# Two pieces of output weights behind the copies of queries, and the clearing of the key buffers tied to the updates: a cross-attention kernel on one core

## What is computed

```python
w     = softmax(x @ rW.T + rb)                       # 8 experts
a_sum = x @ lora_A.T                                 # 64 values
upd   = sum_n w[n] * (a_sum @ lora_B[n].T)
h     = nan_to_num(x + 0.5 * upd)                    # clipped to +-1e4
Q, K, V = h @ Wq.T + bq, ctx @ Wk.T + bk, ctx @ Wv.T + bv
attn  = softmax(where(mask, Q K^T / sqrt(32), -inf))
y     = h + (attn V) @ Wo.T + bo
out   = (y - mean(y)) / sqrt(var(y) + 1e-5) * ln_g + ln_b
```

## Time and profile before

| what | value |
|---|---|
| median of 3 runs | 639.76 us (639.5 to 642.15) |
| the profiled execution's own time | 639.82 us |
| its span | 638.0 us |
| PE busy | 628.6 us, 99% of the span |
| DVE busy | 498.2 us, 78% |
| ACT busy | 337.6 us, 53% |
| POOL busy | 268.0 us, 42% |
| granted TensorE clock | full speed in nearly all of the 40 slices |
| HBM | 67.29 MB read, 46.14 MB written |

### The profile page before, as it was taken

The page is one execution under the profiler, slowest core; times in us unless marked ns, Lnnn a source line. Parts: engine busy times, 40 slices in busy tenths (PEclk is TensorE's granted clock), DMA queues, the critical chain, the costliest instruction groups (busy, mean ns, idle before and its releaser), DMA issues.

```text
span 638.0 us, 10730 instructions
## 1 busy us (share of the span) xinstructions
PE 628.6 (99%) x3455; PEld 544.4 (85%) x3455; DVE 498.2 (78%) x907; ACT 337.6 (53%) x999; POOL 268.0 (42%) x358
## 2 busy tenths in 40 slices
PE   9999999999999999999999999999999999999995
PEld 8988889888988889888788888888888888888884
DVE  5789995578457773677568899999999999999834
ACT  5453453123242232323258777777778777777621
POOL 0120001000030002000325556788899888888956
PEclk9999999999999999999999999999999999999998
DMA  8945595436874467721857993534355354523132
GB/s 316 408 127 173 176 300 190 155 83 205 241 253 160 115 221 246 279 98 38 269 129 282 373 389 107 149 94 148 115 127 179 97 175 111 150 99 117 59 107 100
DMA packets 103399, 114.14 MB, mean 179 GB/s; under 512 B 57008, under 2 KB 76080, under 8 KB 103344
## 3 DMA queue, kind: packets, MB, share of 16 engines
q1 hardware_dynamic: 103008, 113.07, 53.9%
q10 hardware_dynamic: 336, 0.39, 0.2%
HBM read 67.29 MB, written 46.14 MB: 178 GB/s over the span
## 4 chain that ended last, share of the span: by engine, by line
PE 96%; DVE 2%; issue 1%; DMA 0%; ACT 0%; POOL 0%; DVEq 0%; POOLq 0%; ACTq 0%
PE ps L602 26%; PE ps L603 26%; PE ps L604 26%; PE ps L664 4%; PE ps L747 4%; PE ps L760 2%; PE ps L761 2%; PE ps L636 1%; PE ps L638 1%; PE ps L635 1%; PE ps L674 1%; DMA stage<-WkT 0%; DVE u_lo L891 0%; DVE cx_sum L987 0%; PE ps L627 0%
## 5 line engine op out<-in xcount | busy, mean ns | idle before, releaser
L1268 POOL TENSOR_TENSOR u_sb<-a_sb,w_sb 128x512 f32<-128x512 f32 x16 | 19.6, 1246 | 235.3 <-DVE w_sb L885 230.4
L602 PE MATMUL ps<-wo_hi,cx_hi 128*128 128x512 f32 (+1 forms) x264 | 105.9, 401 | 0.0
L1194 ACT ACTIVATE s_sb<-s_sb,s_min 128x64 f32<-128x64 f32 x256 | 85.8, 339 | 34.6 <-DVE s_min L965 34.6
L604 PE MATMUL ps<-wo_hi,cx_lo 128*128 128x512 f32 (+1 forms) x264 | 101.7, 385 | 0.0
L603 PE MATMUL ps<-wo_lo,cx_hi 128*128 128x512 f32 (+1 forms) x264 | 101.6, 385 | 0.0
L602 PE MATMUL ps<-act_hi,w_hi 128*128 128x512 f32 x256 | 100.9, 394 | 0.3 <-DVE q_sb L939 0.3
L603 PE MATMUL ps<-act_lo,w_hi 128*128 128x512 f32 x256 | 99.9, 390 | 0.0
L604 PE MATMUL ps<-act_hi,w_lo 128*128 128x512 f32 x256 | 99.8, 390 | 0.0
L1159 ACT ACTIVATE act_hi<-h_t 128x512 fp32r<-128x512 f32 x32 | 20.3, 633 | 111.6 <-DVE h_t L928 111.6
L987 DVE SCALAR_TENSOR_TENSOR cx_sum<-ps,bias_c,cx_raw 64x256 f32<-64x256 f32 x128 | 61.8, 483 | 8.8 <-ACT cx_raw L1208 4.8
L1279 POOL TENSOR_TENSOR s_sb<-s_sb,s_inv 128x512 f32<-128x512 f32 x64 | 67.1, 1048 | 0.0
(11 more groups left out here) (120 smaller groups left out, 1538.9 us busy)
## 6 DMA issues: line engine op xcount, KB each, us to landing
q_cols<-q_sb SPq DMA_DIRECT2D x32, 512.0 KB, 3.6
qb<-q_cols SPq DMA_DIRECT2D x64, 256.0 KB, 3.9
x_sb<-xT SPq DMA_DIRECT2D x32, 256.0 KB, 3.0
h_rows<-hn_sb SPq DMA_DIRECT2D x64, 128.0 KB, 3.0
output_weights<-wo_sb SPq DMA_DIRECT2D x32, 256.0 KB, 2.7
z_sb<-h_rows SPq DMA_DIRECT2D x16, 512.0 KB, 4.5
out<-z_sb SPq DMA_DIRECT2D x15, 512.0 KB, 2.9
stage<-WvT SPq DMA_DIRECT2D x8, 512.0 KB, 4.7
```

The source lines that it names most:

```text
L602: pe.matmul(dst, lh, rh, start=(first and j == 0), stop=False)
L604: mm = pe.matmul(dst, ll, rh, start=False, stop=(last and j == n - 1))
L1194: act.activation(s_sb[c % 4][:, h, :], s_sb[c % 4][:, h, :], ACT.Exp, bias=s_min[c % 2][:, h:h + 1], scale=-1.0, accum_out=s_sum[c % 2][:, ...
```

## The change

In batches 1 and 2 the seventh piece of output weights no longer stands beside query block 6, ahead of the copies of the queries, but behind them with the eighth. And stage `zero` is no longer between the phases but ahead of `("flush", 3, 6)`, so that ACT's key loads come ahead of its last `add_bias`; POOL's memsets wait for the last update's matmuls (`up_mm`) instead of for the last clipping.

```diff
@@ first_phase
-            for n in range(KC - 1):
+            for n in range(KC - 2):
                 beside[i][n] += [("output_weight", KC * (i - 1) + n)]
...
             if i == NB - 1 and n == 1:
-                return out
+
+                at_flush = out.index(("flush", i, KC - 2))
+                return out[:at_flush] + [("zero",)] + out[at_flush:]
         out += leave(i, 0, 0) + leave(i, 0, 1)
         if 0 < i < NB - 1:
-            out += [("output_weight", KC * i - 1)]
+            out += [("output_weight", KC * i - 2), ("output_weight", KC * i - 1)]
@@ run
-    for what, *index in first_phase() + [("zero",)] + second_phase():
+    for what, *index in first_phase() + second_phase():
@@ zero, on POOL
-                pool.wait_ge(bound_ready, ALL)
+
+                pool.wait_ge(up_mm, ALL)
```

## The result

| | before | after |
|---|---|---|
| median of 20 runs each | 640.34 us | 638.88 us |
| lowest to highest | 639.5 to 642.38 us | 638.27 to 640.27 us |
| span of the profiled execution | 638.0 us | 636.9 us |

The ratio of after to before is 0.9973, with a 95% interval from 0.9965 to 0.9981: 1.7 us faster, between 1.2 and 2.3. It is the ratio of the means; the medians lie 1.46 us apart, since six of the runs of the kernel before lie above 641 us and none of the changed one. I had forecast no change at all, 639.8 us, and so missed a gain that is clear of the noise. The measured median is inside the range and nearest to the rival "no collision", 638.9 us. But the collision took place. The rows tell what came of it.

A forecast was written before the change was run, and what follows sets the result against it. PE was taken to bound the kernel, with 96% of the chain of waits. Output weights -0.64 us plus +0.6 us from the first scores to chunk 4 gave 0.0 us, so 639.8 us, range 638.4 to 641.0.

The forecast's parts named there:

- no collision: Rival: last update's memset and DVE's finite and bound do not clash, first scores start on time; 638.9 us, chance 0.36.
- the collision: At the last update, POOL's third memset shuts out DVE's finite or bound; forecast case 639.8 us, chance 0.47.
- What can be gained at most: PE's stops at batches 1 and 2's second query halves and at the first scores: 1.04 us, 0.16% of the span.
- part 1: Seventh piece of output weights moved behind the query copies: 0.32 us stop gone in batches 1 and 2, -0.64 us.
- Part 2, the collision: Memsets start at about 305.2, 307.0 and 308.7; the third makes DVE's bound of the last update 1.8 us late.
- turns: At the third memset, one of DVE's two instructions slips in at 308.8; the second waits until about 310.9.
- Part 3, the knock-on to the key loads: On ACT, act_hi ends at 313.5, key loads issue 0.3 us later; first scores stop 0.7 us or more, not 0.40.
- What is queued behind: SP stands still 1.5 us before the last h rows; chunk 4's queries land at 334.0, its scores 0.6 us later.
- The SP rival: SP becomes the bound at chunk 4's scores: queries land at 336.0, 2.6 us late; 641.8 us, chance 0.12.
- The sum: Whole kernel: -0.64 from the output weights, +0.6 from first scores to chunk 4, 0.0 us; time stays 639.8 us.
- the collision case: Forecast case with DVE shut out by the third memset: 639.8 us, bounds 639.4 to 640.4, chance 0.47.

The follow-up runs named there:

- Experiment 1: Kernel before with only the seventh piece of output weights moved behind the query copies; memsets and key loads as before: 639.24 us, ratio 0.9982.
- Experiment 5: Changed kernel, but the third memset waits for the last clipping again, the first two stay early: 638.8 us, ratio 0.9976 to the kernel before.
- Experiment 3: Kernel before with only the memsets made early, waiting for the last update's matmuls; key loads stay behind the last add_bias: 641.16 us, ratio 1.0015.
- Experiment 4: Kernel before with only the key loads moved ahead of the last add_bias; memsets still behind the last clipping: 640.03 us, ratio 0.9998.
- experiment 7: Changed kernel with three more loads on SP ahead of the values, waiting for each other: 646.57 us, ratio 1.0095 to the kernel before.

## Why the prediction was right and wrong

- **What can be gained at most** ("1.04 us, 0.16% of the span"): mis-sized. The places were right, all three, and nothing else moved. But I counted the late start of the first matmul only, 0.32 us, and called 1.04 us the most that the change can bring; it brought 1.5 to 1.7. Between two marks with only the first stop between them (the first matmul behind batch 2's transposes of u, and the first behind batch 3's adapter) lie 248.18 - 183.34 = 64.84 us before and 248.04 - 183.72 = 64.32 us after: **0.52 us for a stop**. Behind a stop the next matmul follows after 0.34 us, not 0.23 (186.82 behind 186.48): in a full stream a matmul's weights are loaded beside the matmul ahead of it, and here that load began only 0.11 us after the stopped one, at 186.59. A few hundredths more are lost in the matmuls that follow. At the first scores it is 0.49 us. So part 1 was worth 1.0 us where I had 0.64, and all three 1.5. Experiment 1 measured part 1 at 1.2 us, interval 0.5 to 1.7. The prediction also said that a measurement of this kernel can't tell less than 0.5%, 3.2 us, from no change; with 20 runs of each kernel the interval is 0.5 us to either side, and 1.7 us is well clear of it.
- **Part 2, the collision**: right in place, kind and size (1.67 us for 1.8). Only my "turns" were wrong: it was `finite`, not `bound`, that waited. The two came to the same moment: in all five profiles with the three memsets early and together, the record of `finite` starts at most 0.02 us ahead of that of the third memset, and each time the memset went first. Why it did is not shown. Experiment 5 removed the wait by removing the overlap, so the cause is shown. The row that carried it, DVE and POOL beside each other in the earlier trace rows, was the right one to go by, and the Trainium skill's rule ("SBUF — State Buffer", section "Who interferes with whom") holds in this case: a memset, which only writes, shut out a tensor_scalar until it had ended, 2.10 us against 0.43.
- **Part 3, the knock-on to the key loads**: this is the step that failed. "With DVE 1.8 us late, `act_hi` ends at 313.5, and the loads are issued 0.3 us later than before." They were issued 0.34 us earlier. ACT does not wait for the end of the instruction ahead of a transfer. 0.65 us of error, and with it the sign of the part: the stop went instead of growing. The rows of before could have told: there the loads started 0.08 us after the second memset had ended (311.30 + 1.81 = 313.11), and 0.02 us before `add_bias` had ended by its row (312.48 + 0.73 = 313.21). Experiments 3 and 4 settled it: memset in 4, start of `add_bias` in 3.
- **What is queued behind**: the place was right, the size not. SP paused for 0.38 us instead of 1.5: `add_bias` started 0.65 us sooner than I had it, by the same mistake, and SP itself arrived 0.45 us later, since its two `qb` issues ahead took longer. Then it made up more than it had lost. The stop of 0.6 us ahead of chunk 4's scores was 0.0. That chunk 4's queries are the point where SP would become the bound is shown by experiment 7, and by the 0.22 us that a weight load waited there.
- **The rival "no collision"** gave the right time by luck: its -0.64 was too small by 0.4 us, and its premise did not hold. **The SP rival** did not occur; experiment 7 shows that its mechanism exists and lacks only the delay.
- **The sum**: the two errors both hid a gain, 0.4 us in part 1 and 1.1 us in the rest, together the 1.5 us that I called zero. That the median still lies inside 638.4 to 641.0 is no merit of the mechanism: the range was wide enough for the rival. (Its bounds for the collision case, 639.4 and 640.4, come out at 639.5 and 640.3 by their own terms.)
- **The gaps of PE**: ahead of the prediction "gaps of some 9 us in all" are named. 7.5 us of them lie behind the last matmul (630.5 to 638.0), where DVE, POOL and ACT finish the last rows, 1.2 us ahead of 104.54, and only 0.7 us in all that is between. So the three stops were nearly all that PE's idle time still held there.

Not settled: why the last key load lands 0.6 to 1 us sooner in some profiles. It was not tried to hold the order of the issues on both queues fixed. So how often the stop at the first scores returns in either kernel is known from a few profiles only.

## What to carry to other kernels

Price a stop of a full TensorE by the distance between two marks around it, not by the idle time in front of one matmul: here 0.32 us of late start cost 0.5 us. When an instruction order puts a transfer behind a compute instruction, take the start of that instruction as the transfer's earliest time, and look which semaphore came last before you credit the order. And when an event becomes earlier, look what it now runs beside: the early memsets alone made this kernel 1.0 us slower, through a clash with one short instruction of another engine.

## What the runs showed of the hardware

- A DVE TENSOR_SCALAR that takes 0.43 us alone took 2.10 us when it met a POOL memset of 1.81 us, and went on when that had ended (five profiles; 0.43 again in experiment 5). Beside memsets, DVE's transpose (0.70 us) and its two-input forms (0.65 us) kept their durations.
- A transfer on ACT's queue starts 0.06 to 0.07 us after the start of the activation ahead of it (experiments 3 and 5, and both profiles of the changed kernel), also where that activation takes 0.63 or 0.72 us.
- Within a stop of 5 us TensorE's granted clock fell from 2.4 to 1.2 GHz, and it stayed there for the first 4 us of matmuls behind it, which cost 1.9 us (experiment 7). The stops of 0.3 us did not change the granted clock.
- A PE that waits for a transfer of keys starts 0.09 us after it has landed (five profiles).
- The start of the kernel, up to batch 1's adapter, differed by 2.0 us between profiles of kernels that are the same up to there (104.54 to 106.54 us). It is larger than what was to be measured.
